# The norms of a woven four-layer kernel: their first slot in three parts, and the layout of attention's result as a stage of its own

## The chip, the cores and the metric

One core of one Trainium2 chip runs one launch. The metric is the device time of the launch in microseconds (us). Five engines take part: TensorE (PE; its weight loads are listed as PEld), VectorE (DVE), ScalarE (ACT), GpSimd (POOL) and SyncE (SP), which issues nearly all DMAs.

## The reference, cut to what matters

`x` is 2 x 512 x 144, fp32. Three transformer layers with 16 heads of 9 and a conditioned affine follow each other, then a rotation in a 64-dimensional subspace.

```
for layer in 0, 1, 2:
    shift, scale, gate (x2) = split6(silu(cond) @ W_mod + b_mod)
    h = ln(x) * (1 + scale_a) + shift_a            # norm "msa"
    q, k, v = h @ W_qkv + b ; (layer 1: q, k normalised per head)
    x += gate_a * (softmax(q k' / 3) v @ W_proj + b)
    h = ln(x) * (1 + scale_m) + shift_m            # norm "mlp"
    x += gate_m * mlp(h)                           # layer 0: four experts, top 2; hidden width 576
x + (x U) (R - I) U'                               # U from a QR, R = expm(skew(cond))
ln(h) = (h - mean) * rsqrt(var + 1e-6)
```

## The kernel before

The work is cut into six **blocks**, one for each layer and batch entry (block = 2 * layer + entry). Attention of a block is 64 **steps**: four groups of four heads, 16 steps to a group, each step the scores of one head against 128 keys for all 512 queries. One loop over 384 steps runs on every engine; each engine has its own program, written out in the same order, and they meet at semaphores. In a step, PE (line 1383) makes a score bank, ACT (L797) takes its exponentials, and in each fourth step (n % 4 == 2) PE multiplies four of them with the values (L1422). At n % 16 == 4 PE turns the result of the group before (L1430) and DVE's iteration 5 divides it (`o_normalise`).

The softmax needs each query's **maximum** first. So PE also multiplies queries and keys of the next group in the other order (`max_scores`, L1400) into a ring of three banks, `m_banks`, and DVE reduces each (L972, `take_max`). `TILES[n]` says which of the 16 tiles of the next group belong to step n (mostly one a step, two in the first two, none in the last two), and `BURST_TILES` puts up to four of them beside an MLP stage. At n % 16 == 14 (`TURN_AT`) PE waits until every bank of that ring is drained, turns the maxima (L1409, `max_turn`), and DVE subtracts them from the queries (L979, `place_max`); the scores of step 16 wait for that.

The rest is **woven** between the steps: the stages of the block before (norm "o", proj, norm "mlp", gate, mlp) and of the block after (mods, norm "msa", qkv). A stage has slots; `BANKS_OF` says how many banks of the ring `d_banks` (two banks) each slot takes, and `ROOM` how much room each gets when `slot_steps` spreads the slots of a block over its steps. From `ROOM` and `BANKS_OF` also follow `TILES`, the order of SP's loads and the banks that `KEYS_TURNED` names. PE does the slots of step n at the end of its step n; DVE and ACT do them in iteration n + 1. The solver for U and R is a chain of small steps at fixed places (`SOLVER_PLAN`: a column each 2.5 steps), it takes its bank from the `m_banks` ring as well, and DVE does its part after the slots of the iteration.

A norm is a stage with three slots and room 4, 1, 2. In slot 0 DVE does all of its share for "msa" and "mlp": four `bn_stats` (L1012), one maximum as filling (`fill[0]()`), four `bn_aggr` (L1017), the inverse root in eleven small dependent instructions (L1020, L945, L947 to L949 three times), and four scalings into `h_tok` (L1031). POOL, also in slot 0, takes each scaled tile, multiplies by the scale (L714), adds the shift (L715) and copies the last 16 columns twice (L718). In slots 1 and 2 PE transposes the four tiles (L1454, L1455), two in each; ACT and DVE then make the high and low parts `h_hi`, `h_lo`, `h_d` (L809, L810, L1040, L1043). The kind "o" lays out attention's result with the same stage: DVE has nothing in slot 0 and POOL copies `o_tok` (L717, L718). The kind "x" (before the rotation) has a copy on DVE in slot 0.

The head (`HEAD`) and the tail (`TAIL`) run stages in sequence without steps between them; in the head one solver part follows each slot from slot `HEAD_FROM` on.

Of the kernel before, what the change touches and what calls it, by code (L numbers as in the profile page):

```python
# [84 lines left out]
def stages(block):  # L85

    out = []
    if block == 0:
        out += [("norm", 1, "msa"), ("qkv", 1), ("prep", 1), ("prep", 2), ("mods", 1, 0), ("prep", 3)]
    if block >= 1:  # L90
        out += after_attention(block - 1)
    if block == 1:
        out += [("mods", 1, 1)]
    if block == 2:
        out += [("mods", 2, 0), ("prep", LAYER_ITEM[2])]
    if block == 3:
        out += [("mods", 2, 1)]
    if 1 <= block < BLOCKS - 1:
        out += [("norm", block + 1, "msa"), ("qkv", block + 1)]
    if block == BLOCKS - 1:  # L100
        out += [("norm", block - 1, "x"), ("rotate", 0)]
    return out


def after_attention(block):
    out = [("norm", block, "o"), ("proj", block), ("norm", block, "mlp")]
    if block // B == 0:
        out.append(("gate", block))
    for m in mlps_of(block):
        out.append(("mlp", m, block))  # L110
    return out


HEAD = [("mods", 0, 0), ("mods", 0, 1), ("prep", 0), ("norm", 0, "msa"), ("qkv", 0)]
TAIL = after_attention(BLOCKS - 1) + [("norm", BLOCKS - 1, "x"), ("rotate", 1)]
WOVEN = [st for block in range(BLOCKS) for st in stages(block)]


BANKS_OF = {"prep": (), "mods": (2,), "norm": (0, 2, 0), "qkv": (2, 2, 0, 2, 2, 2, 2), "proj": (2,), "gate": (1, 0),
            "mlp": (7, 0), "rotate": (2,)}  # L120

ROOM = {"prep": (), "mods": (1,), "norm": (4, 1, 2), "qkv": (2, 2, 1, 2, 2, 2, 2), "proj": (2,), "gate": (2, 1),
        "mlp": (1, 1), "rotate": (1,)}
# [36 lines left out]

HEAD_FROM = 3
HEAD_SLOTS = sum(len(BANKS_OF[st[0]]) for st in HEAD)
# [157 lines left out]
def build(nc, a, out):  # L322
    with ExitStack() as ctx:
# [287 lines left out]
        def _(pool):  # L611
# [86 lines left out]
            def norm(blk, kind):  # L698
                b, l = blk % B, blk // B
                mv = mod[:, b, l % 2, :, :]  # L700
                first = 0 if kind == "msa" else 3
                if kind == "o":
                    pool.wait_ge(s["o_taken"], G * (blk + 1))
# [57 lines left out]

            walk = {"norm": norm, "qkv": qkv, "mlp": mlp}

# [20 lines left out]
        def _(act):  # L784
# [18 lines left out]

            def norm(blk, kind):
                yield
                (a_bank, _, _), (d_bank, _, _) = ring.take(), ring.take()
# [84 lines left out]

            walk = {"norm": norm, "qkv": qkv, "gate": gate, "mlp": mlp}

# [37 lines left out]
        def _(dve):  # L931
# [73 lines left out]
            def norm(blk, kind):  # L1005
                b = blk % B
                if kind != "o":
                    if kind == "msa" and blk < B:
                        dve.wait_ge(x_in[b], 16)
                    if kind != "x":  # L1010
# [7 lines left out]
                        done[0] += T  # L1018
                        dve.wait_ge(s["dve_done"], done[0])
                        link(dve.tensor_scalar(nwt[:, 1, 0:T], mean_var[:, :, 1], EPS, None, ALU.add))  # L1020
                        rsqrt(rstd[:, :], nwt[:, 1, 0:T], nwt[:, 0, 0:T])
                    if seen.n.get("norm", 0):
                        dve.wait_ge(s["h_turned"], T * seen.n["norm"])
                    else:
                        dve.wait_ge(s["consts_ready"], 1)
# [143 lines left out]
            def solver(step, taken):  # L1169
# [109 lines left out]
                elif kind == "m":  # L1279
# [7 lines left out]

            walk = {"mods": mods, "norm": norm, "qkv": qkv, "proj": proj, "gate": gate, "mlp": mlp,
                    "rotate": rotate}
# [58 lines left out]
        def _(pe):  # L1348
# [94 lines left out]

            def norm(blk, kind):
                yield
                (a_bank, a_done), (d_bank, d_done) = take(ring), take(ring)
# [122 lines left out]
            def solver(step):  # L1569
# [66 lines left out]
                elif kind == "m":  # L1636
# [8 lines left out]

            walk = {"mods": mods, "norm": norm, "qkv": qkv, "proj": proj, "gate": gate, "mlp": mlp,
                    "rotate": rotate}
# [55 lines left out]
```

## Time and profile before

| | |
|---|---|
| median of 3 runs | 911.35 us (909.35 to 921.39) |
| profiled execution | 919.2 us, span 917.2 us |
| PE busy | 751.5 us, 82% |
| DVE busy | 556.0 us, 61% |
| ACT busy | 386.0 us, 42% |
| POOL busy | 181.0 us, 20% |
| granted TensorE clock, mean | 0.856 |

Busy time is that of the engine's own instructions; a PE row's end is modelled. A row of the timeline gives its start and length in us, its engine, line, operation and tiles, and in brackets how long the engine had been idle before it and which instruction ended that. Each step n starts with the score matmul of line 1383, so the n-th of these rows dates the step. The first stands at 73.6 us, the last at 866.1 us. The blocks take 104.3, 173.9, 178.7, 142.9, 114.4 and 78.4 us of that; before it lies the head, after it the tail.

### The profile page before, as it was taken

The page shows a single profiled execution, that of the slowest core. Times are in us where ns is not written, and L with a number is a line of the kernel's source. Part 1 is how long each engine was busy: PE and PEld are TensorE (multiplying, and loading weights), DVE is VectorE, ACT ScalarE, POOL GpSimd, SP SyncE. Part 2 cuts the span into 40 slices and gives each one's busy share as a digit, 9 for nine tenths or more (in the row PEclk, how much of TensorE's full clock was granted, in tenths as well). Part 3 has the DMA queues.
Part 4 walks back from the last instruction along what each step waited for, and adds up shares of the span by engine and source line. Part 5 has one row for each costly group of instructions (what it writes and reads, how often), then busy time and mean ns, then how long its engine had stood idle before and what let it go on. Part 6 is the DMA issues. An engine that isn't in the chain of part 4 may idle for free.

```text
span 917.2 us, 11092 instructions
## 1 busy us (share of the span) xinstructions
PE 751.5 (82%) x3571; PEld 438.5 (48%) x3571; DVE 556.0 (61%) x1614; ACT 386.0 (42%) x690; POOL 181.0 (20%) x372
## 2 busy tenths in 40 slices
PE   6597889967998799798867886979897789979746
PEld 1353444335764445366444343645443555436325
DVE  3477787886327558752465777474787666785242
ACT  0221465534444544254235442435453356646511
POOL 5502012440132300302323003021003110021020
PEclk9955899989997669799977997976897988999957
DMA  3210100110121000012100000100000101000000
GB/s 88 69 35 7 32 14 22 39 31 13 48 56 32 1 24 13 12 33 60 39 18 1 24 12 13 32 1 1 24 13 11 33 1 25 12 12 1 13 1 13
DMA packets 22714, 21.23 MB, mean 23 GB/s; under 512 B 4831, under 2 KB 17015, under 8 KB 22658
## 3 DMA queue, kind: packets, MB, share of 16 engines
q1 hardware_dynamic: 22610, 20.52, 8.6%
q8 instruction: 29, 0.48, 0.2%
q14 instruction: 27, 0.22, 0.1%
q10 hardware_dynamic: 48, 0.02, 0.0%
HBM read 13.62 MB, written 0.61 MB: 16 GB/s over the span
## 4 chain that ended last, share of the span: by engine, by line
PE 62%; DVE 28%; issue 4%; ACT 2%; POOL 2%; DMA 0%; DVEq 0%; SPq 0%; ACTq 0%; POOLq 0%
PE m_bank L1400 11%; PE o_bank L1422 10%; DVE row_max L972 9%; PE s_bank L1383 8%; PE d_bank L1539 7%; PE d_bank L1483 3%; PE m_bank L1592 3%; PE m_bank L1409 2%; DVE h_tok L1031 2%; PE d_bank L1528 2%; PE d_bank L1440 2%; PE d_bank L1439 1%; PE d_bank L1454 1%; PE d_bank L1530 1%; PE d_bank L1529 1%
## 5 line engine op out<-in xcount | busy, mean ns | idle before, releaser
L797 ACT ACTIVATE probs<-s_bank 128x512 f32<-128x512 f32 x384 | 223.1, 598 | 380.4 <-PE s_bank L1383 377.1
L972 DVE TENSOR_REDUCE row_max<-m_bank 128x1 fp32r<-128x512 f32 x384 | 255.3, 686 | 91.8 <-PE m_bank L1400 86.5
L1400 PE MATMUL m_bank<-k_pad,q_t 128*128 128x512 f32 x348 | 173.1, 511 | 43.0 <-DVE row_max L972 12.6
L1383 PE MATMUL s_bank<-q_t,k_pad 128*128 128x512 f32 x384 | 176.3, 466 | 2.9 <-ACT probs L797 2.0
L1400 PEld LDWEIGHTS m_bank<-k_pad,q_t 128*128 128x128 f32 x348 | 72.1, 212 | 115.0 <-issue 36.8
L1422 PE MATMUL o_bank<-probs,v_aug 128*32 128x512 f32 x768 | 120.6, 704 | 0.7 <-ACT probs L797 0.7
L1383 PEld LDWEIGHTS s_bank<-q_t,k_pad 128*128 128x128 f32 x384 | 81.8, 215 | 30.1 <-ACT probs L797 15.4
L1539 PE MATMUL d_bank<-w,g_act 128*128 128x144 f32 (+1 forms) x480 | 61.8, 288 | 8.7 <-issue 8.7
L1539 PEld LDWEIGHTS d_bank<-w,g_act 128*128 128x128 f32 (+1 forms) x480 | 59.5, 190 | 14.2 <-issue 8.3
L714 POOL TENSOR_TENSOR h_tok<-h_tok,mod 128x144 f32<-128x144 f32 x48 | 23.7, 494 | 202.7 <-DVE h_tok L1031 202.7
L1592 PE MATMUL m_bank<-gram_rows,ident 64*64 64x208 f32 (+42 forms) x128 | 40.3, 403 | 16.0 <-DVE gram_rows L1207 15.6
L876 ACT ACTIVATE g_act<-d_bank 128x512 f32<-128x512 f32 (+1 forms) x60 | 35.5, 598 | 28.6 <-PE d_bank L1531 28.4
L1454 PE MATMUL d_bank<-ident,h_tok 128*128 128x128 f32 x80 | 26.8, 350 | 18.6 <-POOL h_tok L718 18.5
L717 POOL COPY h_tok<-o_tok 128x144 f32<-128x144 f32 x24 | 7.3, 306 | 174.5 <-DVE o_tok L990 174.4
L1409 PEld LDWEIGHTS m_bank<-ident_r,row_max 128*128 128x128 f32 x96 | 15.2, 227 | 47.5 <-issue 26.0
L1409 PE MATMUL m_bank<-ident_r,row_max 128*128 128x128 f32 x96 | 18.7, 325 | 22.4 <-DVE lu L1243 7.7
L742 POOL TENSOR_TENSOR qs_tok<-qkv_tok,qs_tok 128x144 fp32r<-128x144 f32 x24 | 11.4, 475 | 122.9 <-ACT ks_tok L847 122.6
L979 DVE SCALAR_TENSOR_TENSOR q_t<-m_bank,q_t 128x512 fp32r<-128x512 f32 x24 | 16.6, 690 | 31.2 <-PE m_bank L1409 31.2
L1235 DVE TENSOR_SCALAR s_sign<-m_bank 64x1 f32<-64x1 f32 x64 | 9.3, 145 | 41.3 <-PE m_bank L1592 40.7
L1592 PEld LDWEIGHTS m_bank<-gram_rows,ident 64*64 64x64 f32 x128 | 14.3, 157 | 41.6 <-DVE gram_rows L1207 23.5
L1422 PEld LDWEIGHTS o_bank<-probs,v_aug 128*32 128x32 f32 x768 | 16.2, 115 | 37.2 <-issue 32.8
L1528 PE MATMUL d_bank<-h_hi,ff_hi 128*128 128x512 f32 (+1 forms) x60 | 26.5, 442 | 8.6 <-DVE h_d L1043 4.3
(232 smaller groups left out, 1145.1 us busy)
## 6 DMA issues: line engine op xcount, KB each, us to landing
k_pad<-k_t SPq DMA_DIRECT2D x96, 64.0 KB, 2.0
raw_a<-in_L_cond_w_dram SPq DMA_DIRECT2D x10, 288.0 KB
w<-in_L_cond_w_dram SPq DMA_DIRECT2D x10, 288.0 KB
w_rows<-in_L_cond_W_dram SPq DMA_DIRECT2D x8, 141.8 KB
raw_d<-in_L_cond_w_dram SPq DMA_DIRECT2D x30, 36.0 KB
x_tok<-in_x_dram SPq DMA_DIRECT2D x2, 288.0 KB, 4.5
w<-in_L_cond_W_fc_dram SPq DMA_DIRECT2D x2, 288.0 KB
raw_a<-in_L_cond_W_fc_dram SPq DMA_DIRECT2D x2, 288.0 KB
```

The source lines that it names most:

```text
L797: act.activation(probs[:, n % PROBS, :], s_banks[n % S_BANKS][:, :], ACT.Exp, scale=HD ** -0.5)\
L876: act.activation(g_act[rows, f, :], bk[rows, :], ACT.Gelu_apprx_tanh).then_inc(drained, 1)
L972: dve.tensor_reduce(row_max[:, grp % 2, t, MAXROW + 32 * j:MAXROW + 32 * j + 1], bk[:, :], AX.X, ALU.max).then_inc(drained, 1)
L1383: pe.matmul(s_banks[n % S_BANKS][:, :], k_pad[:, grp % PADS, j, kt * P:(kt + 1) * P], q_t[:, par, g, :], start=True, stop=True).then_inc(s ...
L1400: ins = pe.matmul(bk[:, :], q_t[:, par, g, t * P:(t + 1) * P], k_pad[:, grp % PADS, j, :], start=True, stop=True)
L1409: ins = pe.matmul(bk[:, t * P:(t + 1) * P], row_max[:, grp % 2, t, :], ident_r[:, :], start=True, stop=True)
L1422: ins = pe.matmul(o_bank[32 * j:32 * j + 32, :], v_aug[:, par, kt, at:at + 32], probs[:, (GRP * quad + j) % PROBS, :], start=(kt == 0), st ...
L1454: pe.transpose(a_bank[:, cols], h_tok[:, t, 0:P], ident[:, :])
L1483: ins = pe.matmul(bk[:, g * P:(g + 1) * P], src[:, (slot - 3) % 2, g * GRP:(g + 1) * GRP, :] .rearrange("p h w -> p (h w)"), ident_r[:, :] ...
L1528: pe.matmul(bk[0:n, :], ff_hi[:, i, c], h_hi[:, :], start=True, stop=False)
L1539: return pe.matmul(bk[:, t % 2 * C:(t % 2 + 1) * C], g_act[0:k, f, t * P:(t + 1) * P], w2[0:k, i, f, :], start=(f == 0), stop=(f == FT))
L1592: ins = pe.matmul(bk[0:S, j:j + src.shape[1]], ident[0:S, j:j + 1].to_broadcast([S, S]), src, start=True, stop=True)
```

## The change

It does three things. (1) For the kinds "msa" and "mlp" a norm has five slots in place of three. DVE does the statistics in the first, the inverse root in the second, the scalings in the third, and takes one maximum as filling ahead of the second and of the third. POOL's part lies in the third. ACT and PE pass over the first two. (2) The kinds "o" and "x" become a stage "lay", which keeps the three slots of the old norm but has room 2, 1, 2 in place of 4, 1, 2. (3) `HEAD_FROM` goes from 3 to 5, because the head's norm has two more slots; so each solver part of the head stays beside the same slot.

What it adds and takes of instructions: none; the waits are the same ones. The steps to which slots fall, by block (before, then after; the steps count from the block's start):

```
block 0   msa 0,8,10                          msa 0,4,6,10,12
block 1   o 4,7,8   proj 10  mlp 11,15,16     lay 4,5,6   proj 8   mlp 10,11,12,14,15
          msa 28,32,32                        msa 27,29,30,32,32
block 2   as block 1
block 3   o 4,8,9   proj 11  mlp 13,18,19     lay 4,6,7   proj 9   mlp 11,13,14,16,18
          msa 24,28,29                        msa 23,25,26,28,29
block 4   as block 3, msa 23,28,29            as block 3, mlp 11,13,15,17,18, msa 22,25,26,28,29
block 5   o 4,13,15 proj 20  mlp 24,34,36     lay 4,9,11  proj 17  mlp 22,27,30,35,37
          x 45,54,57                          lay 48,53,56
```

The stages of gate, mlp and mods lie one step earlier (block 5's mlp two or three later), the slots of qkv at most one step elsewhere. With them the burst tiles move by one; and SP's load of the third layer's modulation weights stands ahead of that of one expert's weights, behind it before.

```diff
-    out = [("norm", block, "o"), ("proj", block), ("norm", block, "mlp")]
+    out = [("lay", block, "o"), ("proj", block), ("norm", block, "mlp")]
...
-BANKS_OF = {"prep": (), "mods": (2,), "norm": (0, 2, 0), "qkv": (2, 2, 0, 2, 2, 2, 2), "proj": (2,), "gate": (1, 0),
+BANKS_OF = {"prep": (), "mods": (2,), "norm": (0, 0, 0, 2, 0), "lay": (0, 2, 0), "qkv": (2, 2, 0, 2, 2, 2, 2), "proj": (2,), "gate": (1, 0),
...
-ROOM = {"prep": (), "mods": (1,), "norm": (4, 1, 2), "qkv": (2, 2, 1, 2, 2, 2, 2), "proj": (2,), "gate": (2, 1),
+ROOM = {"prep": (), "mods": (1,), "norm": (2, 1, 2, 1, 2), "lay": (2, 1, 2), "qkv": (2, 2, 1, 2, 2, 2, 2), "proj": (2,), "gate": (2, 1),
...
-HEAD_FROM = 3
+HEAD_FROM = 5
...                                                   (POOL, ACT and PE, each in its norm)
+                if kind in ("msa", "mlp"):
+                    yield
+                    yield
...                                                   (DVE)
                         dve.wait_ge(s["dve_done"], done[0])
+                        yield
+                        fill[0]()
                         link(dve.tensor_scalar(nwt[:, 1, 0:T], mean_var[:, :, 1], EPS, None, ALU.add))
                         rsqrt(rstd[:, :], nwt[:, 1, 0:T], nwt[:, 0, 0:T])
+                        yield
+                        fill[0]()
```

## Rows read from the trace of the kernel before

**Rows 1.** The page's first part: busy us (share of span) and instructions of each engine.

```profile
PE 751.5 (82%) x3571; PEld 438.5 (48%) x3571; DVE 556.0 (61%) x1614; ACT 386.0 (42%) x690; POOL 181.0 (20%) x372
```

**Rows 2.** The page's chain that ended last, by engine.

```profile
PE 62%; DVE 28%; issue 4%; ACT 2%; POOL 2%; DMA 0%; DVEq 0%; SPq 0%; ACTq 0%; POOLq 0%
```

**Rows 3.** The page's groups: busy, mean ns | idle before, and its releaser.

```profile
L972 DVE TENSOR_REDUCE row_max<-m_bank 128x1 fp32r<-128x512 f32 x384 | 255.3, 686 | 91.8 <-PE m_bank L1400 86.5
...
L1454 PE MATMUL d_bank<-ident,h_tok 128*128 128x128 f32 x80 | 26.8, 350 | 18.6 <-POOL h_tok L718 18.5
```

**Rows 4.** Timeline of DVE, the mlp norm in block 3: start us, us, what.

```profile
553.85 1.29 DVE L972 TENSOR_REDUCE row_max<-m_bank 128x1 fp32r<-128x512 f32 x2
555.05 0.93 DVE L1012 BATCH_NORM_STATS2 stat<-x_tok 128x6 f32<-128x144 f32 x4
556.02 0.38 DVE L1017 BATCH_NORM_AGGREGATE mean_var<-stat 128x2 f32<-128x6 f32 x4
...
557.03 0.16 DVE L948 TENSOR_TENSOR nwt<-nwt,rstd 128x4 f32<-128x4 f32 x1
...
558.61 1.62 DVE L1031 TENSOR_SCALAR h_tok<-x_tok,mean_var,rstd 128x144 f32<-128x144 f32 x4
```

**Rows 5.** Timeline of PE: six of its ten idle stretches at woven norms.

```profile
81.90 0.80 PE L1400 MATMUL m_bank<-k_pad,q_t 128*128 128x512 f32 x1 [5.12 <-DVE gram_rows L1207]
...
203.36 0.77 PE L1592 MATMUL m_bank<-gram_rows,ident 64*64 64x161 f32 x2 [5.96 <-DVE gram_rows L1207]
...
561.84 0.87 PE L1409 MATMUL m_bank<-ident_r,row_max 128*128 128x128 f32 x3 [5.14 <-DVE rot L1274]
...
698.84 0.80 PE L1400 MATMUL m_bank<-k_pad,q_t 128*128 128x512 f32 x1 [3.98 <-DVE q_t L979]
...
732.72 0.35 PE L1592 MATMUL m_bank<-lu,ident 64*64 64x6 f32 x2 [4.69 <-DVE lu L1243]
...
820.49 0.58 PE L1400 MATMUL m_bank<-k_pad,q_t 128*128 128x512 f32 x1 [3.46 <-DVE row_max L972]
```

**Rows 6.** Windows: length, then PE, PEld, DVE, ACT, POOL busy, PEclk, DMA share, GB/s.

```profile
190.70:203.40 12.70, 5.77 (x35) 3.10 (x34) 11.87 (x40) 2.89 (x6) 2.15 (x5) 0.85 0.20 53
362.90:375.80 12.90, 8.11 (x45) 3.66 (x43) 11.97 (x45) 3.51 (x7) 2.77 (x7) 0.78 0.00 1
547.30:561.90 14.60, 7.49 (x54) 4.33 (x52) 12.78 (x45) 3.09 (x6) 2.57 (x7) 0.98 0.00 1
686.80:699.00 12.20, 6.87 (x42) 4.23 (x40) 11.20 (x43) 2.88 (x5) 1.77 (x5) 0.95 0.09 22
...
649.60:673.30 23.70, 21.38 (x119) 10.84 (x119) 17.82 (x56) 10.03 (x18) 0.00 (x0) 0.93 0.05 12
787.70:799.00 11.30, 11.30 (x56) 5.42 (x56) 9.43 (x17) 7.66 (x15) 1.88 (x8) 1.00 0.10 25
```

**Rows 7.** Windows, same columns: behind the mlp norm of block 3.

```profile
561.40:575.10 13.70, 11.98 (x42) 6.76 (x43) 7.08 (x16) 3.12 (x6) 6.52 (x12) 0.50 0.08 20
```

**Rows 8.** Timeline of POOL and PE at block 4's msa norm.

```profile
730.54 0.49 POOL L714 TENSOR_TENSOR h_tok<-h_tok,mod 128x144 f32<-128x144 f32 x1 [24.15 <-DVE h_tok L1031]
...
734.87 0.41 PE L1454 MATMUL d_bank<-ident,h_tok 128*128 128x128 f32 x1
...
735.51 0.21 POOL L718 COPY h_tok<-h_tok 128x32 f32<-128x32 f32 x1
```

**Rows 9.** Timeline: block 1's step 5 on PE, POOL's weights and its second tile of "o".

```profile
184.28 0.40 PE L1383 MATMUL s_bank<-q_t,k_pad 128*128 128x512 f32 x1
...
185.51 1.40 POOL L693 TENSOR_TENSOR lay_d<-raw_d,lay_d 32x576 fp32r<-32x576 f32 x1
...
187.86 0.21 POOL L718 COPY h_tok<-h_tok 128x32 f32<-128x32 f32 x1
```

**Rows 10.** Timeline: block 2's inverse root on DVE beside POOL's weight preparation.

```profile
456.62 1.40 POOL L693 TENSOR_TENSOR lay_d<-raw_d,lay_d 32x576 fp32r<-32x576 f32 x1
456.80 1.25 DVE L948 TENSOR_TENSOR nwt<-nwt,rstd 128x4 f32<-128x4 f32 x1
```

More of the change, by code:

```diff
@@ L100, in stages @@
     if block == BLOCKS - 1:
-        out += [("norm", block - 1, "x"), ("rotate", 0)]
+        out += [("lay", block - 1, "x"), ("rotate", 0)]
     return out
 def after_attention(block):
-    out = [("norm", block, "o"), ("proj", block), ("norm", block, "mlp")]
+    out = [("lay", block, "o"), ("proj", block), ("norm", block, "mlp")]
     if block // B == 0:
@@ L114 @@
 HEAD = [("mods", 0, 0), ("mods", 0, 1), ("prep", 0), ("norm", 0, "msa"), ("qkv", 0)]
-TAIL = after_attention(BLOCKS - 1) + [("norm", BLOCKS - 1, "x"), ("rotate", 1)]
+TAIL = after_attention(BLOCKS - 1) + [("lay", BLOCKS - 1, "x"), ("rotate", 1)]
 WOVEN = [st for block in range(BLOCKS) for st in stages(block)]
-BANKS_OF = {"prep": (), "mods": (2,), "norm": (0, 2, 0), "qkv": (2, 2, 0, 2, 2, 2, 2), "proj": (2,), "gate": (1, 0),
+BANKS_OF = {"prep": (), "mods": (2,), "norm": (0, 0, 0, 2, 0), "lay": (0, 2, 0), "qkv": (2, 2, 0, 2, 2, 2, 2), "proj": (2,), "gate": (1, 0),
             "mlp": (7, 0), "rotate": (2,)}
-ROOM = {"prep": (), "mods": (1,), "norm": (4, 1, 2), "qkv": (2, 2, 1, 2, 2, 2, 2), "proj": (2,), "gate": (2, 1),
+ROOM = {"prep": (), "mods": (1,), "norm": (2, 1, 2, 1, 2), "lay": (2, 1, 2), "qkv": (2, 2, 1, 2, 2, 2, 2), "proj": (2,), "gate": (2, 1),
         "mlp": (1, 1), "rotate": (1,)}
@@ L760, in solver @@
                     mring.take()
-            walk = {"norm": norm, "qkv": qkv, "mlp": mlp}
+            walk = {"norm": norm, "lay": norm, "qkv": qkv, "mlp": mlp}
             def side(todo):
@@ L804, in norm @@
             def norm(blk, kind):
+                if kind in ("msa", "mlp"):
+                    yield
+                    yield
                 yield
@@ L890, in solver @@
                     act.activation(gram_rows[:, :], bk[0:S, 0:S + C], ACT.Copy).then_inc(drained, 1)
-            walk = {"norm": norm, "qkv": qkv, "gate": gate, "mlp": mlp}
+            walk = {"norm": norm, "lay": norm, "qkv": qkv, "gate": gate, "mlp": mlp}
             def side(todo):
@@ L1019, in norm @@
                         dve.wait_ge(s["dve_done"], done[0])
+                        yield
+                        fill[0]()
                         link(dve.tensor_scalar(nwt[:, 1, 0:T], mean_var[:, :, 1], EPS, None, ALU.add))
                         rsqrt(rstd[:, :], nwt[:, 1, 0:T], nwt[:, 0, 0:T])
+                        yield
+                        fill[0]()
                     if seen.n.get("norm", 0):
@@ L1286, in solver @@
                                             m_d[64:DW, b, :].bitcast(F32), ALU.subtract))
-            walk = {"mods": mods, "norm": norm, "qkv": qkv, "proj": proj, "gate": gate, "mlp": mlp,
+            walk = {"mods": mods, "norm": norm, "lay": norm, "qkv": qkv, "proj": proj, "gate": gate, "mlp": mlp,
                     "rotate": rotate}
@@ L1444, in norm @@
             def norm(blk, kind):
+                if kind in ("msa", "mlp"):
+                    yield
+                    yield
                 yield
@@ L1644, in solver @@
                 last[chain] = ready
-            walk = {"mods": mods, "norm": norm, "qkv": qkv, "proj": proj, "gate": gate, "mlp": mlp,
+            walk = {"mods": mods, "norm": norm, "lay": norm, "qkv": qkv, "proj": proj, "gate": gate, "mlp": mlp,
                     "rotate": rotate}
```

## The prediction

> **What bounds the kernel now.** I read the page's first part: PE is busy 82% of the span, DVE 61% [rows 1]. The chain of waits then says that what ended last is PE for 62% and DVE for 28% [rows 2]. So there are places where PE waits for DVE, and a norm should be one, since DVE's maxima sit in the same queue (255.3 us of them, 0.69 us each) [rows 3]. The timeline of DVE at a norm shows a solid block: statistics from 555.05, aggregates, the eleven small ones, scalings to 560.2 [rows 4], 5.1 us in all. In three parts: A, statistics, 1.35 us (555.05 to 556.40); B, inverse root, 2.2 us (556.40 to 558.61); C, scalings, 1.6 us. PE gets two or three banks ahead and then stands. In the ten norms between steps that idle time is 3.1 to 6.5 us each, 44.7 us together; six of them are in [rows 5]. That is 5% of the run, and the bound of what this change can take straight away. Behind it the clock falls: after the norm of block 3 the granted clock is 0.50 (1.2 GHz) for 13.7 us in which PE is busy 12.0 [rows 7].
>
> But an average hides what a wait costs: is DVE free on either side of its block? The windows from the projection to the release of the turned maxima, blocks 1 to 4, say no: DVE is busy 11.87 of 12.70, 11.97 of 12.90, 12.78 of 14.60 and 11.20 of 12.20 us [rows 6]. PE's idle time there is a lack of DVE time, and cutting the block doesn't make DVE's work less. In steps with nothing but maxima and solver, DVE is busy 17.8 of 23.7 us over 16 steps: 0.37 us free in a step; in block 5's first ten steps 1.9 us free [rows 6].
>
> **The change, part by part.** No instruction and no wait is added; positions move, and the program computes them, so that the change does nothing at all can be left out. Costs are against the profiled 919.2 us (span 917.2 and 2 around it), which is 0.9% over the median of 911.35; I take the difference over unchanged.
>
> *Block 0, msa (A at step 0, B at 4, C at 6).* Before 5.12 us idle [rows 5]. Six steps lie between now, and give DVE 6 x 0.37 = 2.2 us [rows 6]; PE's lead covers a part A. Gain 2.5 us, between 1 and 5.1.
>
> *Blocks 1 and 2, mlp (10, 11, 12).* PE's turning of the maxima at step 14 waits for everything that DVE has before it. DVE reaches C in iteration 13 and a solver part in 14, so A, B and C all still stand before it. The only gain is DVE's free time before: 12.70 - 11.87 = 0.8 and 12.90 - 11.97 = 0.9 us [rows 6], by the projection being two steps earlier. Gain 1.7 us for both.
>
> *"lay" in blocks 1 and 2 (4, 5, 6 in place of 4, 7, 8).* PE now wants two tiles of attention's result behind the scores of step 5, whose matmul starts at 184.28 and ends at 184.7. POOL's second tile is there at 188.07, since POOL still prepares the second layer's weights until 186.9 [rows 9]. That work hangs on SP's load, which waits for a score of block 0's step 47, so it moves along with PE: a wait of 3.4 us in block 1. Everything behind the wait on PE (scores of step 6, thus ACT) is late too. In block 2 POOL is free when DVE has divided; between 0 and 3.4 us, I take 0.8, near the lower end because that cover is absent. Blocks 3 to 5 have a step or more between, cost 0. Together -4.2 us.
>
> *Block 3, mlp (11, 13, 14; the turn at 14).* Here C falls behind the turn: 1.6 us, plus the free 14.60 - 12.78 = 1.8. Then the clock. Of the 12.0 us at 0.50 at most half would go, 6.0; DVE then needs 7.1 + 1.6 = 8.7 of the 13.7 us, so at most 5.0; at least 0, where the idle pieces still bring it down. I take 1.5, near the lower end, since DVE stays busy. Gain 4.9 us.
>
> *Block 4, mlp.* Before, the whole block stood ahead of placing the maxima (3.98 us, ended by L979) [rows 5]. Now C is behind it: 1.6, free time 12.20 - 11.20 = 1.0, clock 1.5 as before. Gain 4.1 us.
>
> *Block 5, mlp (22, 27, 30).* Light steps of 1.13 us; 1.9 us free in ten [rows 6] gives 2.5 in the 13 steps from A on. Idle 3.46 [rows 5] falls to 1.0; the clock, one stretch shorter than block 3's, 1.2 (0 to 2). Gain 3.7 us.
>
> *Blocks 1 to 4, msa.* The idle time of 3.5, 6.5, 3.25 and 4.69 us goes for the most part. What is late next is POOL. In block 4 its four tiles take from 730.54 to 735.72, 5.2 us, and PE came for the first at 734.87, when the last was nearly done [rows 8]. Now between A and C on DVE there come two maxima (0.69 each) and a solver column of about 0.9 us: 2.3 us more before C, while C is two or three short steps ahead of the transposes. So the last tile is 2.3 us later relative to A, and A is one step (about 1 us) earlier. That is -1.3 us a norm at worst, +2 at best, where the clock stays up; I take -0.25 each, -1 us for four.
>
> *Queues.* In POOL's queue only the norm's part moves, with nothing of another stage between its old and its new place. On SP one load pair changes places; the expert's weights are wanted a block later, over 100 us, so this costs 0. If that cover were gone, it would cost a wait for the modulation's end, a few us once. Head and tail have no maxima between slots: 0.
>
> *Sum:* 2.5 + 1.7 - 4.2 + 4.9 + 4.1 + 3.7 - 1.0 = 11.7, say 12 us. 919.2 - 12 = 907; from the median, 899 us.
>
> One thing speaks against placing B elsewhere. Beside a POOL instruction of 456.62 to 458.02 one DVE instruction of 0.16 us took 1.25 and ended at 458.05 [rows 10, 4]. The Trainium skill, "SBUF — State Buffer", section "SBUF: two separate sides", says that a VectorE instruction with two SBUF inputs and a GpSimd instruction that reads SBUF lock the same port pair, and the later one blocks for the whole of the other; by that rule, the trace agrees to 0.03 us.
>
> **The rivals.**
>
> *The full gain (0.20).* Each part is shorter than PE's lead, as in block 5 where the light steps leave DVE air. Then two thirds of 44.7 us go, 30, and 10 us of slow clock: 911 - 40 = 871 us (865 to 887). For it: PE's idle stretches are single long ones [rows 5]. Against: DVE 88 to 93% busy in four windows [rows 6].
>
> *DVE's sum decides everywhere (0.10).* The idle time only falls into pieces, the clock falls as before: 908 to 914 us.
>
> *PE waits for POOL in place of DVE (0.15); the slower side.* Place: the transposes of the eight norms in blocks 1 to 4, and "lay". POOL needs 0.5 + 5.2 us from C's start [rows 8]; if two steps of about 1.3 us pass, PE waits 3 us in each: 24 us, against 2.5 + 3.7 + 1.7 + 4.9 + 4.1 of gains less 4.2: 11 us slower, 923 us (915 to 935). It decides from a wait of 1.5 us per norm on. For it: PE has waited 18.5 us for POOL already [rows 3]. Against: in mlp norms the tiles are wanted one or two DVE-bound steps later, so POOL's time is partly hidden.
>
> *Inverse roots beside POOL's weight preparation (0.05).* Preparation follows the MLP stage, the msa norms too. Two more hits of 1.1 us [rows 10] in each of four: 9 us less gain, 908 us. (This is the port rule above, as this kernel would meet it.)
>
> **How the numbers follow.** The forecast (0.50) has its own range: all upper bounds in clock and msa give 887, all lower ones 914. For 8 in 10 I go down a part of the way into the full gain and up over most of the POOL rival: 880 to 917. Faster by over 2% means below 893.1: the full gain (0.20) and about a quarter of the forecast (0.12). Slower by over 2% means above 929.6: a third of the POOL rival, and something unforeseen, 0.07. About 2% is what a measurement of this kernel tells from no change; its three runs span 1.3%.
>
> **What would show it.** Right: in blocks 1 and 2 idle stretches before L1409 of step 14 that sum to about as before, in two or three pieces; a PE wait of about 3 us for POOL L718 at step 5 of block 1; in blocks 3 and 4 the wait at L1409 or L1400 around step 14 to 16 shorter by 2 us or more; in block 5 none over 1 us; idle time of L1454 for POOL above 18.5 us, some 25 to 30. The full gain would show a total PE idle time down by 30 us and a mean clock above 0.88. The POOL rival: L1454 idle above 40 us. I am wrong if DVE's free time in the steps is not where the parts fall, or if the clock, which I put at 4 us of gain, moves more than that: a mean clock of 0.856 is 2 x 0.144 x 917 = 264 us at 1.2 GHz.

## The result, and the profile after

The changed kernel takes 936.26 us (median of 4 runs, 933.17 to 941.48) against 914.28 us for the one before on the same chip: ratio 1.024, 95% interval 1.015 to 1.033. Run again in five rounds it is 1.017 (1.010 to 1.024). So it is slower, by about 2%; the forecast was 899 us, and the range ended at 917. The kernel before took 919 to 920 us (medians of 17 to 23 runs) beside the later experiments, so the base of the forecast, 911.35 from three runs, was itself some 8 us low; beside it the changed kernel took 932.68. Ratios here compare undisturbed runs alone (one execution of the kernel in which the mlp norms alone are divided, for instance, took 3299 us and is left out), so that a few differ a little from the quotient of the medians.

The profiled execution took 933.17 us, its span 931.2, 14.0 more than before. The page's first part, granted clock by slices, and chain by engine:

```profile
PE 770.3 (83%) x3571; PEld 443.4 (48%) x3571; DVE 556.5 (60%) x1614; ACT 384.7 (41%) x690; POOL 181.1 (19%) x372
...
PEclk9956799987996789799767885969898877999957
...
PE 58%; DVE 26%; POOL 6%; issue 5%; ACT 4%; DMA 0%; DVEq 0%; SPq 0%; ACTq 0%; POOLq 0%
```

The same 3571 matmuls keep PE busy 18.8 us longer than in [rows 1]. PE's idle time, span less busy, only falls from 165.7 to 160.9 us; 18.8 - 4.8 are the 14.0. DVE, ACT and POOL are busy as long as before, within 1.3 us. So the change hardly touched how long PE waits; it made PE's work slower. The throttle's records say how: 294 us of the span at 1.2 GHz in place of 264, mean granted clock 0.842 in place of 0.856. The clock by slices of the kernel before, to lay beside the one above:

```profile
PEclk9955899989997669799977997976897988999957
```

In the chain POOL has 6%, before 2% [rows 2].

The page's groups (busy, mean ns | idle before, and its releaser), for [rows 3]:

```profile
L978 DVE TENSOR_REDUCE row_max<-m_bank 128x1 fp32r<-128x512 f32 x384 | 256.7, 687 | 101.1 <-PE m_bank L1410 95.5
L1410 PE MATMUL m_bank<-k_pad,q_t 128*128 128x512 f32 x348 | 174.6, 515 | 27.4 <-DVE lu L1253 10.9
...
L1467 PE MATMUL d_bank<-ident,h_tok 128*128 128x128 f32 x80 | 28.9, 372 | 33.7 <-POOL h_tok L721 33.5
```

PE's wait for POOL at the transposes goes from 18.5 to 33.5 us. And DVE, whose waits were to go, is now idle 101.1 us ahead of the maxima (91.8 before), for PE. The timeline of the msa norm in block 4, which answers to [rows 8] (start us, us, what, idle time before):

```profile
732.32 0.94 DVE L1018 BATCH_NORM_STATS2 stat<-x_tok 128x6 f32<-128x144 f32 x4
...
735.79 0.16 DVE L1028 TENSOR_SCALAR nwt<-mean_var 128x4 f32<-128x4 f32 x1
...
738.57 1.63 DVE L1041 TENSOR_SCALAR h_tok<-x_tok,mean_var,rstd 128x144 f32<-128x144 f32 x4
739.05 0.49 POOL L717 TENSOR_TENSOR h_tok<-h_tok,mod 128x144 f32<-128x144 f32 x1 [20.78 <-DVE h_tok L1041]
...
740.52 0.45 PE L1467 MATMUL d_bank<-ident,h_tok 128*128 128x128 f32 x1 [3.85 <-POOL h_tok L721]
...
741.71 0.47 PE L1467 MATMUL d_bank<-ident,h_tok 128*128 128x128 f32 x1 [0.53 <-POOL h_tok L721]
...
742.05 0.78 PE L1410 MATMUL m_bank<-k_pad,q_t 128*128 128x512 f32 x1
...
743.05 0.42 PE L1467 MATMUL d_bank<-ident,h_tok 128*128 128x128 f32 x1
...
744.27 0.47 PE L1467 MATMUL d_bank<-ident,h_tok 128*128 128x128 f32 x1 [0.59 <-POOL h_tok L721]
```

Read it from the top. The three parts now stretch from 732.32 to 740.2, with maxima and solver columns between. POOL begins 6.7 us after the statistics, and PE stands before the first tile is there: an idle stretch of 3.85 us for POOL in place of one of 4.69 us for DVE [rows 5], then two short waits for tiles. A max matmul between them takes 0.78 us; at the full clock the same form takes 0.40 to 0.50. The slots of qkv follow.

Slow stretches lie in other places too. Here are two of the changed kernel in block 1, around and behind block 2's msa norm (length, then busy time of PE, PEld, DVE, ACT, POOL, then the clock):

```profile
285.10:302.20 17.10, 15.13 (x47) 7.01 (x40) 10.66 (x33) 4.95 (x10) 4.76 (x13) 0.50 0.11 33
312.40:332.90 20.50, 19.61 (x65) 12.08 (x69) 7.65 (x18) 12.92 (x28) 7.34 (x15) 0.50 0.02 4
```

The kernel before has 3.4 and 6.8 us at 1.2 GHz (from 278.1 and 284.9) where the changed one has the first stretch. The second is no result of the change: the kernel before has its twin,

```profile
305.30:325.80 20.50, 19.63 (x68) 11.78 (x67) 7.20 (x17) 12.61 (x27) 6.74 (x14) 0.50 0.03 6
```

In both PE is busy 96% of the time, at 1.2 GHz.

### The profile page after: what moved, and what is told of

Read it like the earlier page. It is cut to its first block, busy times and chain, and to the rows that moved or that the text cites. A ratio compares the mean times of both kernels' runs of the same rounds, so it can differ in the third digit from the quotient of the medians.

```text
span 931.2 us, 11099 instructions
## 1 busy us (share of the span) xinstructions
PE 770.3 (83%) x3571; PEld 443.4 (48%) x3571; DVE 556.5 (60%) x1614; ACT 384.7 (41%) x690; POOL 181.1 (19%) x372
## 4 chain that ended last, share of the span: by engine, by line
PE 58%; DVE 26%; POOL 6%; issue 5%; ACT 4%; DMA 0%; DVEq 0%; SPq 0%; ACTq 0%; POOLq 0%
PE m_bank L1410 10%; PE o_bank L1432 9%; DVE row_max L978 9%; PE s_bank L1393 7%; PE d_bank L1552 7%; PE d_bank L1496 3%; PE m_bank L1605 3%; PE d_bank L1541 2%; PE m_bank L1419 2%; POOL h_tok L718 2%; PE d_bank L1450 2%; PE d_bank L1449 2%; POOL h_tok L717 2%; DVE gram_rows L1217 1%; PE d_bank L1467 1%
## 5 line engine op out<-in xcount | busy, mean ns | idle before, releaser
L978 DVE TENSOR_REDUCE row_max<-m_bank 128x1 fp32r<-128x512 f32 x384 | 256.7, 687 | 101.1 <-PE m_bank L1410 95.5
L1432 PE MATMUL o_bank<-probs,v_aug 128*32 128x512 f32 x768 | 123.5, 721 | 0.7 <-ACT probs L800 0.7
L1467 PE MATMUL d_bank<-ident,h_tok 128*128 128x128 f32 x80 | 28.9, 372 | 33.7 <-POOL h_tok L721 33.5
L1467 PEld LDWEIGHTS d_bank<-ident,h_tok 128*128 128x128 f32 x80 | 13.4, 167 | 56.9 <-issue 37.7
L1209 DVE RECIPROCAL s_small<-m_bank 64x1 f32<-64x1 f32 x64 | 10.0, 156 | 35.4 <-PE m_bank L1605 34.7
```

Source lines behind the costliest of these rows:

```text
L978: dve.tensor_reduce(row_max[:, grp % 2, t, MAXROW + 32 * j:MAXROW + 32 * j + 1], bk[:, :], AX.X, ALU.max).then_inc(drained, 1)
L1432: ins = pe.matmul(o_bank[32 * j:32 * j + 32, :], v_aug[:, par, kt, at:at + 32], probs[:, (GRP * quad + j) % PROBS, :], start=(kt == 0), st ...
L1467: pe.transpose(a_bank[:, cols], h_tok[:, t, 0:P], ident[:, :])
```

## The experiments

The diffs are against the changed kernel unless they say otherwise. A are the statistics, B the inverse root, C the scalings of a norm; "in place" means that every other slot keeps the step that it has in the kernel before.

**1. The changed kernel again, and its parts by themselves.** The second kernel divides every first slot but leaves all other slots at the steps of before; the third moves them and divides nothing; the fourth keeps the changed kernel's other steps and gives C one step more to the transposes.

```diff
split_in_place   "norm": (2,1,2,1,2), "lay": (2,1,2)   ->   "norm": (1,1,2,1,2), "lay": (4,1,2)
lay_alone        as before, with the stage "lay"; "norm": (4,1,2)  ->  "norm": (5,1,2), "lay": (2,1,2)
split_wide       "norm": (2,1,2,1,2)   ->   "norm": (1,1,3,1,2)
```

> The changed kernel once more, on the chip and beside the runs that the others share. All theories: the ratio of the first measurement, 1.024 (1.015 to 1.033), comes again; about 14 to 20 us over the kernel before.

Measured 1.0168 (1.0100 to 1.0235).

> The norms' first slot in three parts (room 1, 1, 2, 1, 2), but the layouts keep room 4, 1, 2, so that every other slot lies at the step of the kernel before. Theory 'moved stages' (the split costs nothing, the earlier layout, projection and scalings do): 5 to 10 us faster than before. Theory 'split' (three pieces bring the scalings later relative to the transposes, PE waits for POOL, and the slow clock follows): 8 to 20 us slower than before, with idle time of the transposes for POOL about 33 us as in the changed kernel.

Measured 1.0119 (1.0065 to 1.0174); run again with the later ones 1.0100 (1.0066 to 1.0134).

> The opposite corner: all slots at the steps of the changed kernel (layouts with room 2, 1, 2, norms with room 5, 1, 2), but the norm's first slot undivided. Theory 'moved stages': 14 to 20 us slower than before, as the changed kernel or worse. Theory 'split': within 5 us of before, PE's wait for POOL at the transposes near 18 us but for about 3 us at block 1's step 5.

Measured 1.0019 (0.9970 to 1.0067).

> The changed kernel with room 1, 1, 3, 1, 2 in place of 2, 1, 2, 1, 2: statistics, root and scalings one step apart and the transposes three steps behind the scalings in place of two; all other slots as in the changed kernel. Theory 'split' through POOL's lateness: PE's wait for POOL falls by about 8 us and the time by 5 to 10 us against the changed kernel. Theory 'moved stages': no change against it within 5 us.

Measured 1.0060 (1.0020 to 1.0101). So most of the loss is the division's, not the steps': they cost 0.2% by themselves and 0.5 to 0.7% beside the division. And a longer way between scalings and transposes takes a part of it away (PE's wait for POOL 25.0 us in place of 33.5 to 35.4).

**2. One kind of norm at a time.** A stage "cut" with five slots serves the one kind, "norm" with three the other; the rest is at the steps of before.

```diff
+def is_cut(blk, kind):
+    return kind == "mlp"          # msa_alone: kind == "msa"; mlp_and_first: kind == "mlp" or blk == 1
...
-"norm": (2, 1, 2, 1, 2), "lay": (2, 1, 2)
+"norm": (4, 1, 2), "cut": (1, 1, 2, 1, 2), "lay": (4, 1, 2)
```

> Only the five mlp norms between steps are divided in three (room 1, 1, 2, 1, 2), the msa norms stay whole, all other slots at the steps of the kernel before. Theory 'POOL late at msa' (there the transposes come two light steps behind the scalings, and the heavy qkv slots then run at the slow clock): 3 to 14 us faster than before, since the divided kernel in place was shorter by 2 to 5 us in the first 16 steps of blocks 1, 3, 4. Theory 'any division costs': 3 to 8 us slower.

Measured 0.9875 (0.9837 to 0.9914).

> Only the five msa norms between steps are divided, the mlp norms stay whole, all other slots at the steps of the kernel before. Theory 'POOL late at msa': 10 to 22 us slower than before, with PE's wait for POOL at the transposes near 28 us. Theory 'any division costs': 3 to 8 us slower.

Measured 1.0034 (1.0009 to 1.0059), some 3 us, where 10 to 22 was what I held. PE's wait for POOL did grow as expected, to 31.1 us: as much as with both kinds divided. So that wait by itself isn't the loss.

> Once more only the mlp norms divided, in place, for its trace and as partner of the others on this chip. If the division of the mlp norms is good by itself, 0.9875 comes again, 8 to 15 us under the kernel before; the trace should show PE idle time down by 5 to 10 us, and PE's wait for POOL at the transposes under 22 us.

Measured 0.9887 (0.9856 to 0.9918). PE's idle time fell by 3.0 us, not by the 5 to 10 expected, to 162.7; the larger part of the gain is PE's busy time, 743.7 us in place of 751.5. The division of the mlp norms is a gain of 11 us, that of the msa norms a loss of 3. Both together are 1.010 to 1.012, where the sum would be 0.991: some 18 us are in the combination.

> The mlp norms divided in place, and of the msa norms only block 0's, whose transposes lie four steps behind the scalings and whose heavy qkv slots are five further steps away. Both theories: 1 to 4 us under the kernel with the mlp norms alone; the candidate for the best version.

Measured 0.9896 (0.9852 to 0.9939): block 0's msa norm adds nothing that can be told; 1 to 4 us of gain were expected.

> The changed kernel with the msa norms whole again (slots 0, 4 and 5 of the old form at the changed kernel's steps), the mlp norms divided, layouts, projections and mlp norms where the changed kernel has them. Theory 'the divided msa norms carry the loss': 5 to 12 us under the kernel before, 18 to 25 under the changed one. Theory 'the moved steps carry it': 5 us over the kernel before or more, since the division is the good one and only the places differ from the kernel with the mlp norms alone divided.

```diff
 mlp_moved, against mlp_again
-"norm": (4, 1, 2), "cut": (1, 1, 2, 1, 2), "lay": (4, 1, 2)
+"norm": (5, 1, 2), "cut": (2, 1, 2, 1, 2), "lay": (2, 1, 2)
```

Measured 0.9972 (0.9940 to 1.0004). It lies between the two theories: 3 us under the kernel before, not 5 to 12. This is the changed kernel with whole msa norms, and 2% faster than it; but beside divided mlp norms the moved steps cost 0.9% (0.9887 to 0.9972, intervals apart), which they did not by themselves (lay_alone). So the divided msa norms cost 2% wherever the mlp norms are divided too: 0.997 to 1.017 with the moved steps, 0.988 to 1.011 without.

**3. Is POOL's time itself the cause?** In both kernels POOL leaves out the addition of the shift, one of its three instructions on a tile.

```diff
-                        link(pool.tensor_tensor(tile, tile, mv[:, first, :], ALU.add))
```

> The changed kernel, but POOL leaves out the addition of the shift in every msa and mlp norm, so that it needs about 2.9 us for four tiles in place of 5.2. Theory 'POOL late': most of the loss goes, 8 to 15 us under the changed kernel, and its distance from the kernel before with the same left out is under 5 us. Theory 'DVE's pieces alone': 0 to 3 us under the changed kernel.

Measured 0.9924 (0.9895 to 0.9953).

> The kernel before, with the same addition of the shift left out on POOL. Both theories: POOL's tiles come while DVE and PE still work off the solid block, so only 0 to 4 us under the kernel before; it is the partner of the changed kernel with the same left out.

Measured 0.9783 (0.9745 to 0.9821). A shorter POOL gives 2.2% to the kernel before and 2.4% to the changed one. Their distance stays, 0.9924 / 0.9783 = 1.014. That missed what I had expected (8 to 15 us for the changed kernel, 0 to 4 for the one before): POOL's time costs both kernels some 20 us, but it isn't what tells them apart.

**4. Is it the clock?** Ahead of POOL's tiles, in the eight norms of blocks 1 to 4, PE makes 11 unused 128x128 matmuls into the bank that is to be written next. The trace has two rows for each of these calls, 176 in all.

```diff
+WARM = (5, 2, 2, 2)
...
                 for t in range(T):
                     n = seen.next("h_tok_ready")
+                    if (kind == "msa" and blk >= 2) or (kind == "mlp" and blk < BLOCKS - 2):
+                        for _ in range(WARM[t]):
+                            pe.matmul(a_bank[:, 384:512], ident[:, :], ident[:, :], start=True, stop=True)
                     pe.wait_ge(s["h_tok_ready"], n)
```

> The changed kernel with 11 more matmuls (128 x 128, results unused) on PE in the transposes of each of the eight norms of blocks 1 to 4, ahead of each wait for POOL's tile. They are 0.27 us each at full clock, 24 us in all if none is hidden. Theory 'slow clock carries the loss': PE's pauses for POOL are filled, the clock stays up, and the time is 3 to 12 us under the changed kernel in spite of the work. Theory 'waits alone': 3 to 15 us over the changed kernel.

Measured 1.0045 (1.0012 to 1.0078), against 1.0168 without the fill: work was added, and the kernel became faster. The control, the kernel before with the same fill, and the other three:

> The kernel before, with the same 11 unused 128x128 matmuls ahead of the waits for POOL's tiles in each of the eight norms of blocks 1 to 4 (work added, nothing of the result changed). This is the control for the run in which the changed kernel got them. Theory: the waits for POOL are short here (18.5 us in all), so PE wants the time itself, and the added work (up to 24 us at 1.2 GHz, 12 at full) costs more than the clock gives back: ratio 1.005 to 1.02. Rival: filled waits are good for any kernel of this shape, and what they gave the changed one says nothing about the change: 0.98 to 0.995.

Measured 1.0197 (1.0155 to 1.0238).

> The changed kernel with the 11 unused matmuls in each of eight norms, again, on the same chip as the control. Theory: 1.002 to 1.009 as in the first run, so 0.008 to 0.015 below the changed kernel's own ratio of 1.017. Rival (the first result was the chip's): 1.015 or more.

Measured 1.0033 (0.9999 to 1.0068).

> The kernel in which only the mlp norms are divided, every stage where it was before, with the 11 unused matmuls in each of eight norms. Without them its ratio is 0.988. Theory: its waits for POOL are 18.6 us as before, so the fill has little to fill and costs: 0.99 to 1.005. Rival (slow clock behind the msa norms' DVE waits is reached by it too): below 0.985, the best version so far.

Measured 1.0079 (1.0049 to 1.0109), the top of what the theory allowed and a little over.

> All first slots divided, every other slot at the steps of before, a second time, beside the others on one chip. It settles whether the two divisions add up: mlp alone 0.988, msa alone 1.003, sum 0.991. Theory (they don't add: where both norms of a block are divided, PE has no stretch between them in which it catches up with POOL): 1.007 to 1.017 again. Rival (they add, and the first result was the chip's): 0.988 to 0.996.

Measured 1.0100 (1.0066 to 1.0134): the two divisions don't add up, on a second chip as on the first.

> All first slots divided in place (1.010 and 1.012 without the fill) with the 11 unused matmuls ahead of POOL's tiles in each of eight norms. So far the same fill cost the kernel before 2.0% and the one with mlp norms alone divided 2.0%, and gave the changed kernel back 1.3%. Theory (the fill pays where msa norms are divided and PE waits for POOL in them at the lower clock): no cost or a gain, 0.995 to 1.010. Rival (the gain belongs to the changed kernel's other steps): it costs 2% here too, 1.025 to 1.035.

Measured 1.0014 (0.9989 to 1.0038).

> The changed kernel with the unused matmuls in the four msa norms of blocks 1 to 4 alone, half of the fill (1.0033 with all of it, 1.017 without). Theory (it is the msa norms' waits that start the slow stretches, and the fill in the mlp norms costs as it does in the other kernels, about 1%): 0.993 to 1.001. Rival (the mlp norms' waits matter as much): 1.004 to 1.012.

Measured 1.0031 (1.0003 to 1.0059), between the two theories: the same as with the whole fill. The msa norms' half of the fill brings all of its gain; that the other half costs 1%, as I had thought, isn't so.

The same fill in four kernels, ratios to the kernel before. The last column is PE's busy time less that of the fill itself, which is 30.2 to 32.4 us (15.7 in the last row):

| divided | without | with the fill | PE busy without, us | with the fill, less its own |
|---|---|---|---|---|
| nothing (before) | 1 | 1.020 | 751.5 | 740.7 |
| mlp norms | 0.988 | 1.008 | 743.7 | 737.1 |
| both, in place | 1.010 | 1.001 | 766.9 | 733.1 |
| both, changed kernel | 1.017 | 1.003 | 767.2 | 749.8 (fill in the msa norms alone) |

The first two pay 2% for the fill. The last two get 0.9 and 1.3% back, and in the third PE is busy less long in spite of the added work. The rest of PE's work becomes shorter in all four, by 10.8, 6.6, 33.7 and 17.4 us: most by far where both kinds are divided. Three pages, each with PE's line and the group of the transposes: mlp norms divided, without the fill; both in place, without; both in place, with it:

```profile
PE 743.7 (82%) x3571; PEld 434.3 (48%) x3571; DVE 554.8 (61%) x1614; ACT 385.2 (42%) x690; POOL 181.1 (20%) x372
...
L1482 PE MATMUL d_bank<-ident,h_tok 128*128 128x128 f32 x80 | 26.8, 350 | 18.6 <-POOL h_tok L734 18.6
```

```profile
PE 766.9 (83%) x3571; PEld 446.3 (48%) x3571; DVE 555.6 (60%) x1614; ACT 385.1 (41%) x690; POOL 181.6 (20%) x372
...
L1467 PE MATMUL d_bank<-ident,h_tok 128*128 128x128 f32 x80 | 28.4, 368 | 31.2 <-POOL h_tok L721 31.2
```

```profile
PE 765.5 (84%) x3747; PEld 459.2 (50%) x3747; DVE 554.9 (61%) x1614; ACT 384.6 (42%) x690; POOL 181.6 (20%) x372
...
L1471 PE MATMUL d_bank<-ident,h_tok 128*128 128x128 f32 x80 | 24.8, 322 | 22.8 <-POOL h_tok L722 22.7
```

From the first to the second the wait for POOL grows by 12.6 us. PE's idle time as a whole doesn't (162.7 and 161.8 us): the wait for POOL has taken the place of waits for DVE. The whole difference of the spans, 22.3 us, is PE's busy time, 23.2. The kernel with msa norms alone divided has the long wait for POOL too (31.1), and 756.0 us of busy time.

The mean clocks of whole traces can't be compared here: in the second trace no slow stretch is recorded in the first 100 us, although PE is busy 75.06 us there against 73.90 in the first. From 100 us on the mean granted clock is 0.88 in the first of the three, 0.85 in the second and 0.88 in the third; in the kernel before it is 0.87 without and with the fill, with the mlp norms alone divided 0.87 with it, in the changed kernel 0.85 without (0.86 in the second run) and 0.87 with the fill in the msa norms. So the fill raises the clock only where both kinds are divided. From 0.88 to 0.85 is, by an estimate from these means, some 50 us more at 1.2 GHz; at half speed that is some 20 us more of busy time.

**Where it happens.** Block by block the changed kernel is 0.4, 3.5, 4.8, 0.6, 4.3 and 0.4 us longer than the one before. The clearest place is block 4, steps 32 to 47, with six of its seven qkv slots (33 to 43). Windows: before; the changed kernel; the changed kernel with the fill in the msa norms.

```profile
744.10:768.50 24.40, 21.70 (x127) 13.32 (x125) 16.33 (x45) 17.70 (x39) 3.64 (x8) 1.00 0.05 12
```

```profile
753.50:783.40 29.90, 27.69 (x127) 17.16 (x125) 16.26 (x45) 18.23 (x39) 3.64 (x8) 0.77 0.04 10
```

```profile
748.50:772.90 24.40, 21.70 (x127) 13.32 (x125) 16.32 (x45) 17.65 (x39) 3.64 (x8) 1.00 0.05 12
```

The same 127 matmuls at the same steps, and PE's idle time is 2.7, 2.2 and 2.7 us. The loss of 5.5 us is the clock's alone, and the fill ahead of it takes it away whole.

Block 3 can be followed in all kernels. Steps 16 to 31 hold its msa norm (24 to 29), steps 32 to 47 all seven qkv slots. Windows, one fence a kernel: before; mlp norms divided; msa norms divided; both, in place; both, in place, with the fill.

```profile
564.80:614.10 49.30, 41.35 (x202) 24.80 (x200) 29.40 (x88) 17.46 (x28) 8.06 (x16) 0.79 0.08 20
614.10:649.60 35.50, 32.78 (x165) 21.13 (x163) 18.43 (x57) 19.69 (x42) 3.63 (x8) 0.76 0.03 8
```

```profile
557.20:608.60 51.40, 40.71 (x201) 24.58 (x200) 32.15 (x104) 17.21 (x28) 13.24 (x28) 0.80 0.08 20
608.60:640.20 31.60, 28.44 (x165) 18.17 (x163) 18.26 (x56) 19.35 (x42) 3.64 (x8) 0.89 0.04 9
```

```profile
565.70:618.00 52.30, 44.80 (x201) 25.86 (x200) 29.77 (x91) 17.52 (x28) 8.07 (x16) 0.73 0.07 19
618.00:650.70 32.70, 29.52 (x165) 19.11 (x163) 17.86 (x55) 19.27 (x42) 3.64 (x8) 0.86 0.04 9
```

```profile
566.00:621.80 55.80, 44.72 (x201) 26.11 (x200) 32.52 (x107) 17.52 (x28) 13.29 (x28) 0.73 0.07 19
621.80:658.90 37.10, 34.39 (x165) 22.52 (x163) 18.03 (x54) 19.56 (x42) 3.65 (x8) 0.72 0.03 8
```

```profile
560.50:615.10 54.60, 45.22 (x246) 29.21 (x245) 31.72 (x101) 17.54 (x28) 13.31 (x28) 0.84 0.07 18
615.10:643.70 28.60, 25.43 (x166) 16.49 (x164) 18.28 (x57) 19.24 (x42) 3.65 (x8) 1.00 0.04 10
```

The 32 steps take 84.8, 83.0, 85.0, 92.9 and 83.2 us. PE's idle time in them (length less busy) is 10.7, 13.9, 10.7, 13.8 and 12.6: the fourth has no more of it than the second, and is 9.9 us longer. The clock is all of the difference. In the second window the same 165 or 166 matmuls take 34.39 us at a mean clock of 0.72 and 25.43 at 1.00. The trace of the fourth kernel's other run (split_in_place) has the same 55.8 and 37.1 us.

The changed kernel itself does not lose here. Its windows are

```profile
575.00:628.70 53.70, 45.19 (x202) 26.03 (x201) 30.24 (x95) 17.61 (x28) 12.73 (x27) 0.75 0.07 19
628.70:657.80 29.10, 25.92 (x166) 16.92 (x164) 17.81 (x55) 19.15 (x41) 3.64 (x8) 0.98 0.04 10
```

These are 82.8 us, less than in the kernel before. It too has both kinds divided, but at other steps, and loses at other places, such as block 4. So what follows on block 3 is about the kernel with both divided in place.

The stretch at 1.2 GHz that begins at the msa norm lasts 10.2 us in the first kernel (598.9 to 609.1) and in the second, 20.5 in the third, 23.9 in the fourth, 6.9 in the fifth:

```profile
592.70:602.90 10.20, 7.83 (x31) 4.45 (x32) 8.04 (x34) 1.79 (x3) 4.60 (x12) 0.50 0.01 2
```

```profile
599.70:620.20 20.50, 16.91 (x58) 9.09 (x57) 12.69 (x43) 5.33 (x10) 4.61 (x12) 0.50 0.00 1
```

```profile
601.40:625.30 23.90, 20.19 (x72) 11.92 (x73) 13.88 (x50) 5.81 (x11) 4.62 (x12) 0.50 0.00 1
```

```profile
598.70:605.60 6.90, 5.22 (x19) 2.71 (x18) 5.78 (x26) 1.79 (x3) 0.81 (x2) 0.51 0.00 0
```

So a divided msa norm lengthens this stretch here, whether the mlp norms are divided or not. What differs between the third and the fourth is the qkv window behind it: there the third is at a mean clock of 0.86, the fourth at 0.72, with a second stretch of 17.1 us at 1.2 GHz (635.6 to 652.6).

What the fourth has in its stretch are several short idle times of PE, none of them long:

```profile
607.49 0.79 PE L1410 MATMUL m_bank<-k_pad,q_t 128*128 128x512 f32 x1 [1.63 <-DVE lu L1253]
...
610.96 0.45 PE L1467 MATMUL d_bank<-ident,h_tok 128*128 128x128 f32 x1 [1.40 <-POOL h_tok L721]
...
612.15 0.48 PE L1467 MATMUL d_bank<-ident,h_tok 128*128 128x128 f32 x1 [0.53 <-POOL h_tok L721]
```

The undivided norm, in the kernel with mlp norms alone divided, has one idle time there, and its transposes then run without a stop:

```profile
599.38 0.80 PE L1425 MATMUL m_bank<-k_pad,q_t 128*128 128x512 f32 x1 [2.32 <-DVE lu L1268]
```

Its clock rises at 602.9. In the fourth it rises at 625.3, 13 us after the last of the short idle times, though PE is busy all of the time between (13.10 of 13.10 us from 612.2). The Trainium skill, "TensorE: Matmul & The Clock Gate", section "A second HAM failure mode: psum-queue depth-cycling", tells of a kernel in which frequent very short idle times between groups of matmuls make the clock swing between its two levels; this trace agrees as far as idle pieces of 0.5 to 1.6 us lie in 23.9 us at 1.2 GHz. It doesn't show that the pieces hold the clock down: it had fallen at 601.4, ahead of all three, as in the kernel with one long idle time, and outlasted them by 13 us.

## Why the prediction was wrong, step by step

*The frame was right.* That dividing PE's idle time doesn't remove it is what came: 165.7 to 160.9 us of idle time where a full gain would have taken 30.

*The mlp terms* (1.7 for blocks 1 and 2, 4.9, 4.1, 3.7; sum 14.4). Near as a sum, and partly by luck: the mlp norms alone gave 1.1 to 1.25%, some 11 us. The forecast had 10.2 of its 14.4 us in waits and 4.2 in the clock; measured were 3.0 us less idle time and 7.8 us less busy time, so the clock gave most of it and the waits less than a third of what they were to give. By block, in the traces of one execution each, blocks 1 to 5 are 3.0, 0, 6.5, 0.5 and 2.4 us shorter. Block 4's term was too large; its idle time in steps 16 to 31 rose from 9.0 to 12.8 us. In block 3 of the changed kernel the stretch ahead of the turn, 5.14 us in [rows 5], is less than half:

```profile
572.06 1.08 PE L1419 MATMUL m_bank<-ident_r,row_max 128*128 128x128 f32 x4 [2.19 <-DVE rot L1284]
...
575.94 0.45 PE L1467 MATMUL d_bank<-ident,h_tok 128*128 128x128 f32 x1 [0.32 <-POOL h_tok L721]
...
577.13 0.47 PE L1467 MATMUL d_bank<-ident,h_tok 128*128 128x128 f32 x1 [0.53 <-POOL h_tok L721]
```

Yet all of these matmuls lie in a stretch at 1.2 GHz (568.4 to 585.5). In steps 0 to 15 of block 3 the changed kernel's idle time fell from 9.4 to 5.7 us, by what the term had for the wait (1.6 + 1.8); but its busy time rose from 25.0 to 30.2, where the term had a gain of 1.5 for the clock. In block 5 the wait went too (steps 16 to 31 are 4.9 us shorter), but steps 32 to 47, where the MLP's slots lie two or three steps later, are 4.7 us longer, and the 3.7 us are not to be seen in the changed kernel.

*Block 0's msa norm* (2.5): not seen; 0.9896 with it and 0.9887 without, each uncertain by 0.4%.

*"lay"* (-4.2, of it 3.4 in block 1). I had forecast a wait of about 3 us for POOL at step 5. It is 1.60:

```profile
185.35 0.40 PE L1393 MATMUL s_bank<-q_t,k_pad 128*128 128x512 f32 x1
187.35 0.30 PE L1467 MATMUL d_bank<-ident,h_tok 128*128 128x128 f32 x1 [1.60 <-POOL h_tok L721]
187.49 0.27 PE L1468 MATMUL d_bank<-ident,h_tok 128*96 128x128 f32 x1
```

POOL's weights were done 1.7 us earlier here than in [rows 9] (183.83 + 1.40 against 185.51 + 1.40), and attention's result came later, at 186.2, so that DVE and not POOL set most of it. All moved steps together cost 0.2% by themselves, which can't be told from nothing (experiment 1), but 0.9% beside divided mlp norms (experiment 2). The forecast took the two for independent.

*The msa norms of blocks 1 to 4* (-1.0; at worst -1.3 each, -5 for four). This is the step that failed. The mechanism was named: maxima and solver parts come between A and C, the transposes stand two or three short steps behind C, POOL becomes what is late. By itself the term isn't far off: 0.3%, some 3 us. But I added it to the mlp terms as if they were independent, and beside divided mlp norms it costs 2.0 to 2.2%, 18 to 20 us. I priced it as waiting time, one wait taking another's place, and idle time as a whole did not grow (162.7 and 161.8 us). The clock I had only as a gain "where it stays up", never as a loss. In its place the runs show a loss that is all PE's busy time, 23.2 us at an equal count of matmuls, and slots of qkv at a lower clock: 27.69 us in place of 21.70 in block 4 of the changed kernel.

*The clock* (4 us of gain, in the mlp norms alone). Named as what could be wrong, and it was, in sign too: 294 us at 1.2 GHz in place of 264, PE's busy time 18.8 us up. I took shorter idle stretches to be better for it than long ones; [rows 7] gave me the price of a slow stretch, but no row told what makes one last, and at that point I should have asked what a stretch that lasts into qkv costs.

*The POOL rival* (0.15; 923, range 915 to 935). It has the right sign and the right place, and its upper end, 935, is near the result. But its own sign, a wait above 40 us, did not come (33.5), experiment 3 says that POOL's time isn't the difference, and with the msa norms alone divided the same wait (31.1) goes with a loss of 0.3%. That its number comes near is luck. The forecast was for a wait of 25 to 30.

*The other rivals.* The full gain (871 us) and "DVE's sum decides" (908 to 914) did not come. Nor did the inverse roots beside POOL's preparation: the changed kernel has one instruction of them at 1.25 us, as the kernel before has.

*What stays open.* Why the chip's clock stays low in one kernel and not in another was shown only as far as this: fill the waits, and it comes back. Why mlp and msa divisions cost so much only together is not known. In place, it is block 3 (146.2 us against 136.8 by adding), block 0 (105.7 against about 100) and block 1 (170.9 against 167) that differ, and of these only block 3 was followed; in the changed kernel it is other slots. The two traces of the kernel with both divided in place differ by 3.4 us in block 0 and 6.3 in block 1 (and not in block 3), so a single trace says little of those two. The kernel with msa norms alone divided was not run with the fill. And the fill's gain in blocks 1 to 4 couldn't be split further: with the msa norms alone it was the same as with all eight.

The best of all versions is the one with the mlp norms alone divided, in place: 0.988, 909.4 against 919.07 us, faster than both kernels, without any of the fill.

## What to carry to other kernels

Before dividing a block of work that another engine waits for, price the pieces not only as waiting time but by what PE does right behind them, at either level of its clock: here 16 dense steps took 24.40 us at the one and 29.90 with a part at the other. And don't add the prices of two divisions that meet in one chain of steps before they have been measured together. Where a chain ends in per-tile hand-overs (here DVE, POOL, PE), leave room between its last part and its consumer, or leave it whole. And when a kernel has changed, compare PE's busy time at an equal count of instructions before any wait: here it rose by 18.8 us while idle time fell by 4.8, and that tells where to look.

## What the runs showed of the hardware that was not expected

- PE busy 96% of 20.5 us (19.61 us, 312.4 to 332.9; 19.63 in the kernel before) while the granted clock was 0.50: a busy engine isn't by itself a fast one.
- Unused matmuls in waits can pay: 176 rows of them, some 31 us of PE's busy time, took 1.2 to 1.4% off the changed kernel, and put 2.0% onto the one before.
- One of POOL's three instructions on a tile (0.49 us, 12 norms of four tiles, 23.3 us busy in all) is worth 2.2 and 2.4% of the time, 20 us: nearly its full length, though POOL is busy only 20% of the span. POOL takes 0.49 us for a 128x144 addition where DVE takes 0.46 for a 128x288 one:

```profile
729.53 0.46 DVE L1085 TENSOR_TENSOR x_tok<-x_tok,gated 128x288 f32<-128x288 f32 x1
...
739.62 0.49 POOL L718 TENSOR_TENSOR h_tok<-h_tok,mod 128x144 f32<-128x144 f32 x1
```

The Trainium skill, "GPSIMD Engine Reference", section "Elementwise — side-by-side cycle accounting", has a two-input fp32 addition of 2048 elements 1.96 times slower on GpSimd than on VectorE; by these two rows, of different and smaller sizes, it is 2.1 times for each element, so they agree nearly. A version with this addition on another engine was not tried.
